# The last batch's two norms and its store, written out apart at the end of the experts stage

## The chip, the cores and the metric

The kernel runs on one core of one Trainium2 chip. The metric is the device time of one execution in microseconds. The kernel before took 1379.23 us (median of three runs, 1375.58 to 1379.28).

## The reference

Four residual blocks run one after the other over x, of 16 batches of 512 tokens of width 128: attention, a gated feed-forward, a state-space block with its own feed-forward, and a mixture of experts. Only the end of the last one matters here:

```python
spikes_moe = sigmoid(output_flat @ c2s_W + c2s_b)
decoded = sigmoid(spikes_moe @ dec_W + dec_b)
y = (decoded - mean(decoded)) * rsqrt(var(decoded) + 1e-5) * ln_g + ln_b
x = x + (y - mean(y)) / sqrt(var(y) + 1e-5)
```

Both means and variances go over the 128 features of a token. `ln_g` and `ln_b` have one value per feature, so they are applied between the two norms.

## The kernel before

Tokens lie on the 128 partitions: a batch is four tiles (NT = 4) of 128 tokens by 128 features, kept in `X[:, u]` (the residual stream) and `Y[:, u + 1]` (what is to be added). Names: PE is the tensor engine, DVE VectorE, ACT ScalarE, POOL GpSimd, SP the queue that issues the stores.

The stage is `experts()`. Each engine has its own program, written as `body(i, ...)` and driven by `rounds()` (L1981): rounds 0 to 3 written out, rounds 4 to 11 in a hardware loop of two rounds a turn, rounds 12 to 19 written out (B = 16). In round i the engines work on several batches at once: batch i is encoded and routed, batch i - 1 goes through its experts, batch i - 2 is decoded (flag `c`) and its first norm is measured, batch i - 3 goes through the affine part and its second norm is measured (flag `shapes`), and batch i - 4 is added and stored (flag `ends`). `parts()` (L1975) turns the flags off at the ends of the stage. So the last batch, u = 15, is decoded in round 17, shaped in round 18, and added and stored in round 19. Within a round the order of each engine's instructions is the order in the code, and semaphores couple the engines.

The path of one batch u from its decode to its store:

- ACT writes the sigmoid of the decoder's output to `Y` (L2110).
- DVE measures the first norm (`moments_of`, L149 to L163): four `bn_stats`, then five small instructions, of which the last writes `var4`.
- POOL turns `var4` into 1/sqrt (`invert`, L202 to L210: a power and a Newton step, five instructions each waiting for the one before) and makes `offsets` = neg * rstd (L236).
- ACT applies scale and offset to the four tiles (`normalise`, L2066).
- POOL multiplies by the gain and adds the bias (`shape`, L2019 and L2022).
- DVE measures the second norm, POOL inverts it and makes offsets, ACT applies them, all as above.
- POOL adds Y to X (`add`, L2013), and SP stores the batch in one DMA of 256 KB (L1998), which the stage's end waits for.

POOL's round has the order: `shape(i - 3)`, `add(i - 4)`, `shaped.invert` and offset of batch i - 3, `decoded.invert` and offset of batch i - 2. ACT's round 17 has the order: `normalise` of batch 14 by its first norm, two spikes activations (L2088), the sigmoid of batch 15 (L2110), and `normalise` of batch 14 by its second norm. DVE's round 17 measures the second norm of batch 14 and then the first of batch 15.

The instruction order that the change touches on POOL:

```python
if shapes:
    shaped.invert(pool, i - 3, shaped.rstd)
    shaped.offset(pool, i - 3)
if c:
    decoded.invert(pool, i - 2, decoded.rstd)
    decoded.offset(pool, i - 2)
```

Of the kernel before, what the change touches and what calls it, by code (L numbers as in the profile page):

```python
# [14 lines left out]
ALU = mybir.AluOpType  # L15
ACT = mybir.ActivationFunctionType
# [38 lines left out]
class Core:  # L55
# [25 lines left out]
    def sem(self, name):  # L81
        return self.ctx.enter_context(self.nc.semaphore(name))
# [1839 lines left out]
def experts(core, I, W, store):  # L1922
# [8 lines left out]
    with ExitStack() as ctx:  # L1931
# [24 lines left out]
        normed, summed = [[sem(f"{n}{k}") for k in ("x", "y", "z")] for n in ("normed", "summed")]  # L1956
        out = store.rearrange("b (c p) d -> p b c d", p=P)
        stored = sem("stored")
        spread_over = lambda a: a[:].unsqueeze(1).to_broadcast([P, NT, D])
        gap_done, share_done, gates_done = sem("gap_done"), sem("share_done"), sem("gates_done")  # L1960

        heard = sem("heard")
        FIRST_XT = 1
        logits_use, dec_use, next_xT_use = (lambda i, k=k: i * 3 + k for k in (2, 3, 4))
        decoded_use = lambda i, a, b: i * 3 + (3 if a else 2 if b else 0)
# [9 lines left out]
        def parts(i):  # L1975

            within = lambda lo, hi: not isinstance(i, int) or lo <= i <= hi
            return dict(a=within(0, B - 1), b=within(1, B), c=within(2, B + 1), more=within(0, B - 2),
                        joins=within(0, B - 4), shapes=within(3, B + 2), ends=within(4, B + 3))

        def rounds(eng, body):  # L1981

            for i in range(4):
                body(i, i % 2, **parts(i))
            with eng.Fori(0, (B - 8) // 2) as j:
                for p in range(2):
                    i = j * 2 + (p + 4)
                    body(i, p, **parts(i))
            for i in range(B - 4, B + 4):
                body(i, i % 2, **parts(i))  # L1990

        @block.sync
        def _(sp):
            def body(i, p, ends, **_):
                if ends:
                    sp.wait_ge(summed[2], i - 3)
                    sp.sem_inc(core.turns, 1)
                    sp.dma_start(out[:, i - 4], X[:, i - 4]).then_inc(stored, 16)  # L1998

            rounds(sp, body)  # L2000
            sp.wait_ge(stored, 16 * B)

        @block.gpsimd
        def _(pool):
            layer_norm = lambda b: pool_norm(core, pool, b, xn, core.xmean, core.xrstd, centred, b + 1, xn_done)
            pool.memset(rT[64:65], 1.0).then_inc(init, 1)
            pool.wait_ge(init, 1)
            pool.memset(gates[:], 0.0).then_inc(init, 1)

            def add(u, k):  # L2010
                pool.wait_ge(normed[k], u + 1)
                pool.sem_inc(core.turns, 1)
                pool.tensor_tensor(X[:, u], X[:, u], Y[:, u + 1], ALU.add).then_inc(summed[k], 1)  # L2013

            def shape(u):
                y = Y[:, u + 1]
                pool.wait_ge(normed[1], u + 1)
                pool.sem_inc(core.turns, 1)
                pool.tensor_tensor(y, y, spread_over(W.gain), ALU.mult).then_inc(summed[1], 1)  # L2019
                pool.wait_ge(summed[1], u * 2 + 1)  # L2020
                pool.sem_inc(core.turns, 1)
                pool.tensor_tensor(y, y, spread_over(W.bias), ALU.add).then_inc(summed[1], 1)  # L2022

            joined.constant(pool, init, 2)
            add(0, 0)
            add(1, 0)
            joined.invert(pool, 0, core.xrstd)
            layer_norm(0)
            joined.invert(pool, 1, core.xrstd)
            add(2, 0)  # L2030
            pool.wait_ge(TP.full, FIRST_XT)
            pool.sem_inc(core.turns, 1)
            layer_norm(1)

            def body(i, p, c, more, joins, shapes, ends, **_):
                if shapes:
                    shape(i - 3)
                if ends:
                    add(i - 4, 2)
                if isinstance(i, int) and i == 0:  # L2040
                    joined.invert(pool, 2, core.xrstd)
                if joins:
                    add(i + 3, 0)
                if more:
                    pool.wait_ge(TP.full, next_xT_use(i))
                    pool.sem_inc(core.turns, 1)
                    if not isinstance(i, int) or i < B - 2:
                        layer_norm(i + 2)
                if shapes:
                    shaped.invert(pool, i - 3, shaped.rstd)  # L2050
                    shaped.offset(pool, i - 3)
                if c:
                    decoded.invert(pool, i - 2, decoded.rstd)
                    decoded.offset(pool, i - 2)
                if joins:
                    joined.invert(pool, i + 3, core.xrstd)

            pool.wait_ge(*W.experts)
            rounds(pool, body)

        @block.scalar
        def _(act):
# [18 lines left out]
            def spikes_encoded(n, m):  # L2081
                EB[m].read(act, n)
                EB[m].emptied(act.activation(enc[:, m], EB[m].t[:], ACT.Sigmoid, bias=W.encb[:, m:m + 1]))
# [8 lines left out]
                    HB[h].read(act, n)  # L2092
                    HB[h].emptied(act.activation(hid[:, 2 * k + h], HB[h].t[:], ACT.Relu))  # L2093

            def body(i, p, a, b, c, more, joins, shapes, **_):
                if a:
                    FB.read(act, cont_use(i))
                    act.activation(rT[0:64], FB.t[router], ACT.Tanh, bias=s2rb[:]).then_inc(heard, 1)
                if shapes:
                    decoded.wait(act, i - 3)  # L2100
                    normalise(i - 3, decoded.rstd, decoded.offsets, normed[1])
                if c:
                    cells_to_spikes(c2s_use(i))
                if joins:
                    normalise(i + 3, rstd, shift, normed[0])
                if b:
                    expert_hidden(hid_use(i, 0), 0)
                if c:
                    TP.read(act, decoded_use(i, a, b))
                    TP.emptied(act.activation(Y[:, i - 1].rearrange("p c d -> p (c d)"), TP.t[:], ACT.Sigmoid))  # L2110
                if b:
                    expert_hidden(hid_use(i, 1), 1)
                if more:
                    take_xT(next_xT_use(i))
                if a:
                    act.wait_ge(gap_done, i + 1)
                    act.activation(share[:], gap[:], ACT.Sigmoid).then_inc(share_done, 1)
                if b:
                    expert_hidden(hid_use(i, 2), 2)
                if more:  # L2120
                    spikes_encoded(next_enc_use(i), 0)
                if b:
                    expert_hidden(hid_use(i, 3), 3)
                if more:
                    spikes_encoded(next_enc_use(i), 1)
                if shapes:
                    shaped.wait(act, i - 3)
                    normalise(i - 3, shaped.rstd, shaped.offsets, normed[2])

            act.wait_ge(W.folded, W.MERGED)  # L2130
            take_xT(FIRST_XT)
            for m in range(HC):
                spikes_encoded(1, m)
            rounds(act, body)

        @block.tensor
        def _(pe):
# [142 lines left out]

        @block.vector
        def _(v):
            tick = Tally(v, steps, per=14)
            wide = lambda a: a.unsqueeze(2).to_broadcast([P, NT, E])
            numbers = W.number.unsqueeze(1).to_broadcast([P, NT, E])

# [31 lines left out]
            def gate(i):  # L2318
                slots = lambda a, n: gates[:, :, a * E:(a + n) * E].rearrange("p c (s e) -> p c s e", e=E)
                copies = lambda n: hit[:].unsqueeze(2).to_broadcast([P, NT, n, E])  # L2320
                v.wait_ge(share_done, i + 1)
                v.tensor_tensor(hit[:], mask[0][:], wide(share[:, 0]), ALU.mult)
                tick.step(v.tensor_tensor(cand[:], mask[1][:], wide(share[:, 1]), ALU.mult))
                tick.step(v.tensor_tensor(hit[:], hit[:], cand[:], ALU.add))
                tick.step(v.tensor_copy(slots(0, 3), copies(3)))
                v.tensor_tensor(hit[:], hit[:], gates[:, :, 0:E], ALU.subtract).then_inc(gates_done, 1)
                v.wait_ge(gates_done, i * PARTS + 1)
                v.tensor_copy(slots(3, 2), copies(2)).then_inc(gates_done, 1)
                v.wait_ge(gates_done, i * PARTS + 2)
                v.tensor_tensor(gates[:, :, 5 * E:6 * E], hit[:], gates[:, :, 3 * E:4 * E], ALU.subtract)\  # L2330
                 .then_inc(gates_done, 1)

            def body(i, p, a, b, c, joins, shapes, **_):
                if a:
# [48 lines left out]
            v.wait_ge(W.shaped, W.SHAPED)  # L2383
            v.wait_ge(init, 2)
            rounds(v, body)


def program(nc, I, out):
# [65 lines left out]
```

## Time and profile before

| | us |
|---|---|
| median of 3 runs | 1379.23 |
| lowest, highest run | 1375.58, 1379.28 |
| the profiled execution, its own time | 1381.35 |
| its span, first to last instruction | 1379.2 |
| last matmul of the kernel (PE L2227) ends | 1357.2 |
| last add on POOL (L2013) ends | 1376.45 |

Busy shares of the span: PE 86%, DVE 69%, ACT 66%, POOL 48%. Times in the rows are microseconds from the start of the span. Engine names with a q behind them (POOLq, SPq) are an engine's sequencer, which issues DMAs and holds waits. "Idle before <- X" says how long an engine stood still before an instruction and what released it.

### The profile page before, as it was taken

How to read it: one execution, taken by the hardware profiler on the slowest of the kernel's cores; microseconds unless marked ns; L12 is line 12 of the kernel's file. 1: busy time of each engine (PE TensorE's matmuls, PEld its weight loads, DVE VectorE, ACT ScalarE, POOL GpSimd, SP SyncE). 2: the span in 40 equal slices, each digit the busy share in tenths (PEclk: the TensorE clock that was granted, in tenths of full speed). 3: DMA queues.
4: the chain of work that ended last, by engine and by line, in shares of the span. 5: the costliest groups of instructions: out<-in, count | busy, mean ns of one | idle time of the engine just before them, and what ended most of it. 6: DMA issues, size and time to landing. Idle time of an engine off the chain costs nothing. (4 is left out here: it accounts for less than half of the span.)

```text
span 1379.2 us, 27741 instructions
## 1 busy us (share of the span) xinstructions
PE 1186.9 (86%) x7410; PEld 529.1 (38%) x7410; DVE 946.4 (69%) x2936; ACT 912.9 (66%) x1373; POOL 668.7 (48%) x1127
## 2 busy tenths in 40 slices
PE   3698999999999999993999568999669999999993
PEld 1122222222222222222656458677423433434431
DVE  3477777777777777673799676566545788888752
ACT  2588999999999999994455590333424666666553
POOL 5444555565555555433355541122242566666545
PEclk8699999999999999996999879999869999999997
DMA  4664565555555555507810011000000000000000
GB/s 119 132 117 90 99 112 108 107 108 102 104 108 105 107 100 100 104 1 191 246 36 0 1 63 62 1 0 0 0 0 0 9 9 15 15 8 16 16 16 23
DMA packets 71177, 87.95 MB, mean 64 GB/s; under 512 B 10136, under 2 KB 64958, under 8 KB 65214
## 3 DMA queue, kind: packets, MB, share of 16 engines
q1 hardware_dynamic: 69078, 85.55, 29.8%
q10 hardware_dynamic: 2024, 1.51, 0.5%
q8 instruction: 33, 0.54, 0.2%
q14 instruction: 42, 0.34, 0.1%
HBM read 63.84 MB, written 31.59 MB: 69 GB/s over the span
## 5 line engine op out<-in xcount | busy, mean ns | idle before, releaser
L511 ACT ACTIVATE a_probs<-a_S 128x1024 f32<-128x1024 f32 x512 | 496.6, 1036 | 74.0 <-DVE a_S L653 66.0
L653 DVE TENSOR_TENSOR a_S<-a_S,a_tables 128x256 f32<-128x256 f32 (+1 forms) x512 | 281.1, 560 | 157.3 <-PE a_S L527 154.4
L534 PE MATMUL a_O<-a_probs,a_V 128*32 128x512 f32 x2048 | 275.1, 609 | 2.4 <-ACT a_probs L511 0.6
L527 PE MATMUL a_S<-a_Qs,a_Ks 48*128 48x512 bf16 x1024 | 180.0, 388 | 26.8 <-DMA a_Qs<-a_parts_dram 13.9
L527 PEld LDWEIGHTS a_S<-a_Qs,a_Ks 48*128 48x128 bf16 x1024 | 42.7, 93 | 242.2 <-ACT a_probs L511 196.1
L2093 ACT ACTIVATE e_hid<-e_H 128x512 f32<-128x512 f32 x128 | 69.5, 595 | 61.5 <-PE e_H L2199 61.5
L431 POOL CAST a_parts<-a_whole 128x512 bf16<-128x512 f32 x47 | 29.1, 620 | 157.6 <-DVE a_whole L663 148.2
L1843 ACT ACTIVATE g_hid<-g_H,w_b 128x512 f32<-128x512 f32 x64 | 44.0, 687 | 84.2 <-PE g_H L1866 84.2
L2197 PE MATMUL e_H<-e_gated,w_We 64*128 64x512 f32 x256 | 74.2, 656 | 1.3 <-ACT e_hid L2093 1.2
L534 PEld LDWEIGHTS a_O<-a_probs,a_V 128*32 128x32 f32 x2048 | 40.4, 108 | 82.6 <-issue 67.4
L2208 PE MATMUL e_O<-e_hid,w_We 128*64 128x512 f32 x256 | 69.5, 615 | 0.4 <-ACT e_hid L2093 0.4
L2300 DVE TENSOR_TENSOR e_gated<-e_contT,e_G 128x512 f32<-128x512 f32 x64 | 43.8, 684 | 25.3 <-PE e_G L2189 25.0
L1866 PE MATMUL g_H<-g_ynT,w_w 128*128 128x512 f32 x128 | 60.4, 617 | 0.9 <-DVE g_ynT L1308 0.9
L1876 PEld LDWEIGHTS g_OUT<-w_w,g_hid 128*128 128x128 f32 x512 | 59.7, 192 | 0.6
L550 PE MATMUL a_M<-ident,a_Osb 128*128 128x128 f32 x256 | 41.8, 286 | 21.1 <-DVE a_xnT L657 17.2
L1876 PE MATMUL g_OUT<-w_w,g_hid 128*128 128x128 f32 x512 | 59.7, 275 | 0.0
L440 POOL TENSOR_TENSOR a_parts<-a_whole,a_parts 128x512 bf16<-128x512 f32 x47 | 54.5, 1161 | 8.6 <-POOL a_parts L437 8.6
L434 POOL TENSOR_TENSOR a_whole<-a_whole,a_parts 128x512 f32<-128x512 f32 x47 | 54.4, 1158 | 8.6 <-POOL a_parts L431 8.6
L1495 PE MATMUL f_OUT<-f_wT,f_hid 128*128 128x128 f32 x384 | 49.4, 288 | 6.1 <-ACT XY L1420 6.1
L202 POOL TENSOR_TENSOR g_power_rstd<-g_power_var,g_power_half (+1 forms) x16 | 16.3, 1018 | 76.7 <-DVE g_power_var L179 76.5
L1495 PEld LDWEIGHTS f_OUT<-f_wT,f_hid 128*128 128x128 f32 x384 | 46.7, 200 | 12.8 <-ACT XY L1420 9.4
L550 PEld LDWEIGHTS a_M<-ident,a_Osb 128*128 128x128 f32 x256 | 26.8, 140 | 56.1 <-issue 30.1
(357 smaller groups left out, 2412.0 us busy)
## 6 DMA issues: line engine op xcount, KB each, us to landing
a_parts_dram<-a_parts SPq DMA_DIRECT2D x94, 192.0 KB, 5.7
a_Qs<-a_parts_dram SPq DMA_DIRECT2D x64, 192.0 KB
a_Qs<-a_parts_dram SPq DMA_DIRECT2D x64, 128.0 KB
m_taps_by_step<-h_taps SPq DMA_DIRECT2D x8, 1024.0 KB, 13.6
m_taps<-m_taps_by_step SPq DMA_DIRECT2D x8, 1024.0 KB, 5.0
a_Ks<-a_parts_dram SPq DMA_DIRECT2D x30, 192.0 KB
XY<-L_attn_x SPq DMA_DIRECT2D x16, 256.0 KB, 7.2
a_Qs<-a_parts_dram SPq DMA_DIRECT2D x64, 64.0 KB
```

What stands on the lines that cost most here:

```text
L440: pool.tensor_tensor(part(2), whole[w][:], part(1), ALU.subtract).then_inc(lowered[w], 1)
L511: act.activation(probs[n % KEPT][:], S[n % RING][:], ACT.Exp).then_inc(exped, 1)
L527: mm = pe.matmul(S[n % RING][:, par, :], Ks[p][rows, pr, kb * P:(kb + 1) * P], Qs[p][Q_OF(kb)][rows, pr, :], start=True, stop=True)
L534: mm = pe.matmul(O[VC * j:VC * (j + 1), :], V[q][:, kb, HG * g + j, :], probs[(2 * m + j // 2) % KEPT][:, j % 2, :], start=(kb == 0), stop ...
L550: mm = pe.transpose(M[:, tile_of(core, c)], src[:, tile_of(core, c)], core.ident[:])
L653: v.tensor_tensor(s[:, :, where], s[:, :, where], wide, ALU.mult).then_inc(corrected, 1)
L1495: mm = pe.matmul(OUT[q].t[:, tile_of(core, c)], hid[q][:, m, tile_of(core, c)], wT[2][:, m, :], start=(m == 0), stop=(m == FC - 1))
L1866: pe.matmul(H[m][:], w1[:, tile_of(core, m)], ynT[p][:], start=True, stop=True).then_inc(h_full, 1)
L1876: mm = pe.matmul(o, hid[p][:, m, tile_of(core, c)], w2[:, m, :], start=False, stop=(m == FC - 1), skip_group_check=True)
L2093: HB[h].emptied(act.activation(hid[:, 2 * k + h], HB[h].t[:], ACT.Relu))
L2197: pe.matmul(HB[h].t[:], W.We1[half[h], k], gated[k % 2][half[h]], start=True, stop=False)
L2208: mm = pe.matmul(OB.t[h * M:(h + 1) * M], W.We2[:, 2 * k + h, :], hid[:, 2 * k + h, :], start=(k == 0 and h == 1), stop=(k == PAIRS - 1), ...
```

## The change

Batch 15 leaves the common rounds after its decode. The rounds end at 18, `shapes` ends with round 17 and `ends` with round 18, and POOL does nothing more for batch 15. In round 17 ACT, behind the sigmoid of batch 15, loads the table for the square root and takes the root of the first norm's variance (`root(0, decoded)`), ahead of its `normalise` of batch 14; the root of the second (`root(1, shaped)`) comes behind the rounds. DVE has a new function `close(15)` behind its rounds: four instructions (y + neg) * gain, a reciprocal of the root, four y * rstd + bias, the measuring of the second norm, four y + neg, a reciprocal, and four y * rstd + x. All of the four-fold ones are 128x128 instructions, one for each tile. SP and ACT each issue one half (two tiles, 128 KB) of the store of batch 15, both waiting for the last of DVE's steps.

```diff
+        GAINED, BIASED, MOVED, CLOSED = (PER * B + n for n in (2, 3, 4, 6))
+        CHAIN = Norm.MEASURE * B
+        roots = sb("roots", [P, 2, NT])
...
-                        joins=within(0, B - 4), shapes=within(3, B + 2), ends=within(4, B + 3))
+                        joins=within(0, B - 4), shapes=within(3, B + 1), ends=within(4, B + 2),
+                        closes=isinstance(i, int) and i == B + 1)
...
-            for i in range(B - 4, B + 4):
+            for i in range(B - 4, B + 3):
...
             rounds(sp, body)
-            sp.wait_ge(stored, 16 * B)
+            sp.wait_ge(steps, CLOSED)
+            sp.dma_start(out[:, B - 1, 0:NT // 2], X[:, B - 1, 0:NT // 2]).then_inc(stored, 16)
+            sp.wait_ge(stored, 16 * (B + 1))
...
-                if c:
+                if c and not closes:
                     decoded.invert(pool, i - 2, decoded.rstd)
                     decoded.offset(pool, i - 2)
...
+                if closes:
+                    act.preload_act_table(ACT.Sqrt)
+                    root(0, decoded)
                 if shapes:
                     shaped.wait(act, i - 3)
                     normalise(i - 3, shaped.rstd, shaped.offsets, normed[2])
+
+            def root(k, norm):
+                act.wait_ge(norm.steps, norm.start + CHAIN)
+                act.activation(roots[:, k], norm.var4[:, B - 1], ACT.Sqrt, scale=0.25).then_inc(normed[1], 1)
...
             rounds(act, body)
+            root(1, shaped)
+            act.wait_ge(steps, CLOSED)
+            act.dma_start(out[:, B - 1, NT // 2:NT], X[:, B - 1, NT // 2:NT]).then_inc(stored, 16)
...
+            def close(u):
+                y, x = Y[:, u + 1], X[:, u]
+                last = Tally(v, steps, start=PER * B)
+                for c in range(NT):
+                    op = v.scalar_tensor_tensor(y[:, c], y[:, c], decoded.neg[:, u, c:c + 1], W.gain[:], ALU.add, ALU.mult)
+                last.mark(op)
+                v.wait_ge(normed[1], B)
+                last.step(v.reciprocal(decoded.rstd[:, u], roots[:, 0]))
+                assert last.start + last.n == GAINED
+                for c in range(NT):
+                    op = v.scalar_tensor_tensor(y[:, c], y[:, c], decoded.rstd[:, u, c:c + 1], W.bias[:], ALU.mult, ALU.add)
+                last.step(op)
+                assert last.start + last.n == BIASED
+                shaped.moments_of(v, u, y)
+                for c in range(NT):
+                    op = v.tensor_scalar(y[:, c], y[:, c], shaped.neg[:, u, c:c + 1], None, ALU.add)
+                last.mark(op)
+                assert last.start + last.n == MOVED
+                v.wait_ge(normed[1], B + 1)
+                last.step(v.reciprocal(shaped.rstd[:, u], roots[:, 1]))
+                for c in range(NT):
+                    op = v.scalar_tensor_tensor(x[:, c], y[:, c], shaped.rstd[:, u, c:c + 1], x[:, c], ALU.mult, ALU.add)
+                last.mark(op)
+                assert last.start + last.n == CLOSED
...
             rounds(v, body)
+            close(B - 1)
```

## Rows read from the trace of the kernel before

**Rows 1.** The page: the chain that ended last, shares of the span by engine.

```profile
DVE 10%; PE 10%; issue 4%; POOL 1%; ACT 1%; DVEq 1%; POOLq 0%; ACTq 0%
```

**Rows 2.** The chain that ended last, 1358 to the end: start us, us, what.

```profile
1358.15 1.03 POOL e_shaped_rstd L202
...
1361.07 0.97 POOL e_decoded_rstd L202
...
1363.94 1.66 ACT XY L2066 x4
...
1365.77 1.27 POOL XY L2019
...
1368.50 0.89 DVE e_shaped_st L149 x4
...
1375.16 1.29 POOLq L1931
```

**Rows 3.** Timeline, 1357 to 1369: start us, us, engine, line, instruction.

```profile
1357.25 0.60 ACT L2110 ACTIVATE XY<-e_TP 128x512 f32<-128x512 f32 x1 [2.30 <-PE e_TP L2227]
...
1357.89 0.86 DVE L149 BATCH_NORM_STATS2 e_decoded_st<-XY 128x6 f32<-128x128 f32 x4
...
1359.33 0.16 DVE L163 SCALAR_TENSOR_TENSOR e_decoded_var<-e_decoded_spread,e_decoded_square 128x4 f32<-128x4 f32 x1
...
1361.10 1.65 ACT L2066 ACTIVATE XY<-XY,e_shaped_offsets,e_shaped_rstd 128x128 f32<-128x128 f32 x4 [3.26 <-POOL e_shaped_offsets L236]
...
1368.42 1.26 POOL L2013 TENSOR_TENSOR XY<-XY 128x512 f32<-128x512 f32 x1
```

**Rows 4.** Stores and other DMAs: issue ns, KB each, us from issue to landing.

```profile
L1998 SPq DMA_DIRECT2D out<-XY x16: 378/380/416, 1096.6 to 1376.5; - x16
...
DMA to landing us min/median/max: 2.3/2.3/2.3
a_parts_dram<-a_parts ACTq DMA_DIRECT2D x2, 192.0 KB, 2.8
XY<-L_attn_Wk ACTq DMA_DIRECT2D x1, 64.0 KB, 2.1
```

**Rows 5.** DVE on 128x128 operands: one line's durations (ns min/median/max), two timeline groups.

```profile
L738 DVE SCALAR_TENSOR_TENSOR XY<-XY x15: 339/343/593, 94.0 to 113.8; 128x128 f32<-128x128 f32 x15
643.45 1.10 DVE L1516 TENSOR_SCALAR f_xn<-XY,xmean,xrstd 128x128 f32<-128x128 f32 x4
859.84 0.87 DVE L1887 TENSOR_SCALAR g_yn<-XY,g_power_rstd 128x128 f32<-128x128 f32 x4 [0.32 <-POOL g_power_rstd L210]
```

**Rows 6.** Groups by shape, DVE: a reciprocal (busy us, mean ns | idle before).

```profile
L715 DVE RECIPROCAL XY<-XY 128x16 f32<-128x16 f32 x1 | 0.2, 247 | 0.0
```

**Rows 7.** Timeline of ACT around two table loads, and the work behind each.

```profile
779.99 1.28 ACT L1451 ACT_TABLE_LOAD   x1
...
795.24 10.88 ACT L1701 ACTIVATE m_u<-XY,in_rstd,urstd 128x128 f32<-128x128 f32 x28 [1.92 <-DVE in_mean L1754]
992.25 1.28 ACT L2071 ACT_TABLE_LOAD   x1
...
993.54 4.72 ACT L2066 ACTIVATE XY<-XY,e_shift,e_rstd 128x128 f32<-128x128 f32 x12
```

**Rows 8.** Timeline of POOL and DVE at two places where their work overlaps.

```profile
1323.13 1.27 POOL L2013 TENSOR_TENSOR XY<-XY 128x512 f32<-128x512 f32 x1
1323.25 1.19 DVE L2309 SCALAR_TENSOR_TENSOR e_cand<-e_hit,w_table 128x32 f32<-128x32 f32 x1
92.20 1.04 POOL L99 TENSOR_TENSOR a_xn<-XY,in_mean 128x512 f32<-128x512 f32 x1 [0.27 <-POOL in_rstd L210]
92.69 0.63 DVE L736 TENSOR_SCALAR XY<-XY 128x128 f32<-128x128 f32 x1
```

**Rows 9.** One line's durations (ns min/median/max), and one of the page's instruction queues.

```profile
L2309 DVE SCALAR_TENSOR_TENSOR e_cand<-e_hit,w_table x32: 191/191/1278, 1016.9 to 1325.6; 128x32 f32<-128x32 f32 x32
q8 instruction: 33, 0.54, 0.2%
```

More of the change, by code:

```diff
@@ L1958, in experts @@
         stored = sem("stored")
+        PER = 14
         spread_over = lambda a: a[:].unsqueeze(1).to_broadcast([P, NT, D])
@@ L2033, in _, with body @@
             layer_norm(1)
-            def body(i, p, c, more, joins, shapes, ends, **_):
+            def body(i, p, c, more, joins, shapes, ends, closes, **_):
                 if shapes:
@@ L2093, in expert_hidden, with body @@
                     HB[h].emptied(act.activation(hid[:, 2 * k + h], HB[h].t[:], ACT.Relu))
-            def body(i, p, a, b, c, more, joins, shapes, **_):
+            def body(i, p, a, b, c, more, joins, shapes, closes, **_):
                 if a:
@@ L2282, in _ @@
         def _(v):
-            tick = Tally(v, steps, per=14)
+            tick = Tally(v, steps, per=PER)
             wide = lambda a: a.unsqueeze(2).to_broadcast([P, NT, E])
```

## The prediction

> **What bounds the kernel now.** I read the page first. Its chain of work that ended last gives PE and DVE a tenth of the span each and POOL and ACT a hundredth each [rows 1]: the end of the kernel is small beside the rest, and nothing the change does can be worth more than that end. So I went to the same chain in order of time, from 1358 us on [rows 2]. The last matmul is over at 1357.2, and from there only DVE, ACT and POOL pass one batch from hand to hand: POOL begins to invert batch 15's first norm at 1361.07, ACT applies it at 1363.94, POOL does gain and bias from 1365.77 on, DVE measures the second norm at 1368.50, and POOL's final add goes from 1375.16 to 1375.16 + 1.29 = 1376.45. No other work stands between these steps. The timeline [rows 3] shows where the handing over starts: ACT's sigmoid of batch 15 ends at 1357.25 + 0.60 = 1357.85, and DVE has its first variance ready at 1359.33 + 0.16 = 1359.49. Everything before 1359.49 is the same in both kernels. From there to 1376.45 are 16.96 us, and the store and the end of the program take 1379.2 - 1376.45 = 2.75 us more, of which 2.3 are the store's way from issue to landing [rows 4]. These 19.7 us are all that the change can touch.
>
> **What goes.** Batch 15's inversions on POOL (each a power of about 1.0 us and five short steps, 2.9 us in all, 1361.07 to 1363.94), the wait of the first one behind the inversion of batch 14 (1359.49 to 1361.07), two four-tile passes on ACT of 1.65 us, and three POOL passes of about 1.27 us, one of which, the bias, had also to run before DVE could measure.
>
> **What comes, on DVE.** The trace has the same form, a `scalar_tensor_tensor` of 128x128 with a per-partition scalar and two inputs in SBUF: line 738, median 343 ns [rows 5]. It never stands there four in a row. The nearest group of four, with two per-partition scalars, takes 1.10 us for four where one takes about 336 ns, so one starts every 0.255 us; I take 1.10 us for each group of four. The `tensor_scalar` group with one scalar takes 0.87 us [rows 5]. The lower bound for a group is 0.87, the upper is four unoverlapped, 4 x 0.343 = 1.37. The reciprocal of 128x4 is not in the trace; the one of 128x16 takes 247 ns [rows 6], that is its upper bound, and I take 0.2. Step by step:
>
> - The first group starts behind the variance's issue, at 1359.41, and ends at 1359.41 + 1.10 = 1360.51.
> - The reciprocal runs to about 1360.65. It waits for ACT's root. ACT is free at 1357.85, the table load takes 1.28 [rows 7] and ends at 1359.13, the root waits for 1359.49 and is done by 1359.75: 0.7 us of cover. If this cover were gone, each 0.1 us would count in full.
> - y * rstd + bias: to 1361.75, and 0.03 to see it written: 1361.78.
> - The second norm is measured as the first one was, 1357.89 to 1359.49 = 1.60 us [rows 3]: 1363.38.
> - The four y + neg start with the variance's issue, 1363.30 + 0.87 = 1364.17. ACT's second root (0.2 us) lies beside them, behind ACT's pass over batch 14, which ends at 1361.10 + 1.65 = 1362.75 [rows 3].
> - Reciprocal to 1364.31, the last four to 1365.41.
>
> That is 1376.45 - 1365.41 = 11.04 us earlier, if nothing is in DVE's way.
>
> **What is in its way.** POOL's add of batch 14, which before ran at 1368.42 behind the gain and bias of batch 15 [rows 3], now waits only for ACT's pass, and so starts at about 1362.75 + 0.18 = 1362.93, right in DVE's close. Rows show what that does: an add of POOL from 1323.13 to 1324.40 held a DVE instruction with two SBUF inputs, started at 1323.25, until 1324.44, 1.19 us instead of the line's median 0.191 [rows 8, 9]; a one-input `tensor_scalar` of 128x128 was held in the same way, 92.69 to 93.32, by POOL's work to 93.24 [rows 8]. The neg of the second norm, which has two inputs, is due 1.6 - 0.16 - 0.27 = 1.17 us behind 1361.78, at 1362.95, just as the add sets in. In the rows the held instructions began 0.15 to 0.2 us before the recorded end of POOL's (1324.44 - 0.19 = 1324.25; 93.32 - 0.28 = 93.04), so the neg would begin at about 1364.19 - 0.17 = 1364.02, **1.07 us** late, and all behind it. If the add came a little later it would hit y + neg or the last four instead, at about the same price, as all of them are of the forms held in the rows. Lower bound 0 (DVE is first each time, or the add falls on `bn_stats`), upper 1.26, one add. The close then ends at 1366.48.
>
> The Trainium skill, page "SBUF — State Buffer", section "Who interferes with whom", has a rule that speaks against this change: a DVE instruction with two SBUF inputs and a GpSimd instruction that reads SBUF lock each other out for a whole instruction, and whoever comes first wins. The rows above show one direction. No row here shows POOL held up by DVE.
>
> **Elsewhere on the queues.** ACT's table load and first root stand ahead of its pass over batch 14. That pass started at 1361.10, and ACT is free again at 1359.75, so it hides them with 1.35 us to spare. The pass uses Identity: after the load for the square root at 779.99 ACT ran Identity passes with no second load [rows 7], so I count none. The Trainium skill, page "ScalarE: Activation LUTs", section "What ACT_TABLE_LOAD costs", gives about 1.38 us of drain on top of the load, 2.66 us in all. Here the trace disagrees: the load at 992.25 ends at 993.53 and the next pass starts at 993.54 [rows 7]. By the page the first root would come at about 1360.75, DVE's reciprocal 0.3 us late, and the gain 0.3 us smaller. The sum goes by the row.
>
> The store: SP has its store of batch 14 (issue 0.38 us) ahead of the half, issued near 1364.3 and out of the way. The two halves of 128 KB move the same bytes at once. No row has a 128 KB store; a 64 KB load takes 2.1 us and a 192 KB store from ACT's queue 2.8, against 2.3 for the whole batch [rows 4]. So the halves gain at most 0.2 us and lose at most 0.5; nearest is the 256 KB store itself, and I take 0 and leave the 2.75 us as they are.
>
> **Sum.** 11.04 - 1.07 = 9.97, say **10.0 us** earlier. The profiled execution took 1381.35 us, of which 1379.2 span and 2.15 around it; it becomes 1371.35. The median of the runs lies 2.12 below that execution, so the forecast for the median is 1379.23 - 10.0 = **1369.2 us**, 0.7% less. A measurement of this kernel can tell about 0.3%, 4.1 us, from no change.
>
> **The rivals.**
>
> 1. No collision: the gain is 11.0, 1368.2 us. For it: the neg and the add meet within 0.02 us in my sum, and either could win; against: the add has then still y + neg and the last four to meet. Chance 0.22.
> 2. The lock works both ways. POOL's short steps for batch 14, which end at 1361.07 now [rows 2], then have to find room between DVE's two groups; only the stretch of `bn_stats` from 1361.78 is free. The offset comes at about 1362.7, ACT's pass ends at 1364.4, the second root is done at 1364.65, 0.5 us after DVE could have used it, and the add of batch 14 meets the last four. DVE ends near 1366.8, or POOL's add ends at 1367.0 and SP issues batch 14's store ahead of the last half. The gain is 8.7 to 9.7; at 9.2, 1370.0 us. For it: the same lock; against: POOL's power of about 1.0 us at 1358.15 [rows 2] did not hold DVE's small two-input instructions up to 1359.49. By the rule of the Trainium skill cited above (whoever comes first wins), this is what happens if DVE is first. Chance 0.20.
> 3. No difference that can be measured: DVE's groups cost their upper bounds (3 x 0.27 more), the add collides, the halves lose 0.5, and some 4 us of fetching or waiting come that I don't see; 1375 to 1379. Chance 0.04.
> 4. **Slower: the straight code is fetched late.** The place is the close on DVE, some 36 instructions executed once, behind a loop. The price of one stop is at least that of a small transfer, 2.1 us [rows 4]. It decides from the point at which the stops cost more than 10.0 + 4.1 = 14.1 us, seven in a row: 1383.9 us. Against it: the first instruction queue needed 33 packets for the whole kernel [rows 9], and rounds 12 to 19 are straight code too and show no such gap on the chain. Chance 0.02. With 0.01 for the runs' own scatter this gives 0.03 for slower.
> 5. That the change does not do what it says: the last four could run while the end is set elsewhere, but the chain shows no other work behind 1357.2 than batches 14 and 15, so it is part of rival 2.
>
> **How the numbers follow.** The forecast has 0.51, rivals 1 and 2 have 0.42, all of them faster by over 0.3%; 0.04 for the same, 0.03 for slower. The range takes the gains from 8.7 to 11.0 and the scatter of the runs: low 1375.58 - 11.0 = 1364.6, high 1381.35 - 8.7 = 1372.7.
>
> **What would show it.** In the profile after: (a) DVE's variance of batch 15's first norm at 1359.5, then a close of 6.0 to 7.1 us; (b) groups of four at 1.10 and 0.87 us; (c) one table load of 1.28 us on ACT ending before DVE's first group does, and no second one; (d) the add of batch 14 within the close, and one DVE instruction beside it of over 1 us; (e) 2.75 us from the last DVE instruction to the end. The prediction is wrong if the span shrinks by less than 8.7 us, if DVE waits for a root, or if POOL's add is the last work before the store.

## The result and the profile after

The changed kernel took 1368.46 us (median of five runs, 1367.31 to 1371.03), the kernel before 1379.28 (five runs, 1375.58 to 1380.87). The ratio is 0.9928, with a 95% interval from 0.9914 to 0.9942: 9.9 us faster, between 8.0 and 11.9. The profiled execution took 1368.46 us, with a span of 1366.4 us, 12.8 us less than the one before.

The chain that ended last, from 1355 us to the end, is all DVE now, but for 0.26 us of DVE's sequencer (start us, us, what); in the kernel before POOL, ACT and DVE took turns there [rows 2]:

```profile
1356.57 0.16 DVE e_decoded_var L163
1356.73 1.05 DVE XY L2354 x4
1357.78 0.10 DVE e_decoded_rstd L2357
...
1357.90 1.15 DVE XY L2360 x4
...
1359.08 0.88 DVE e_shaped_st L149 x4
...
1360.53 0.16 DVE e_shaped_var L163
1360.69 1.79 DVE XY L2365 x4
1362.48 0.10 DVE e_shaped_rstd L2369
...
1362.60 0.35 DVE XY L2371
1362.95 0.26 DVEq L1931
1363.22 0.52 DVE XY L2371 x2
```

The timeline of the same stretch shows what the other engines did beside it:

```profile
1355.09 1.28 ACT L2134 ACT_TABLE_LOAD   x1
...
1356.57 0.16 DVE L163 SCALAR_TENSOR_TENSOR e_decoded_var<-e_decoded_spread,e_decoded_square 128x4 f32<-128x4 f32 x1
...
1356.65 1.13 DVE L2354 SCALAR_TENSOR_TENSOR XY<-XY,e_decoded_neg,w_gain 128x128 f32<-128x128 f32 x4
1356.77 0.20 ACT L2142 ACTIVATE e_roots<-e_decoded_var 128x4 f32<-128x4 f32 x1 [0.40 <-DVE e_decoded_var L163]
1356.98 0.34 POOL L206 TENSOR_TENSOR e_shaped_work<-e_shaped_work,e_shaped_var 128x4 f32<-128x4 f32 x1 [0.18 <-POOL e_shaped_work L204]
...
1357.70 0.17 DVE L2357 RECIPROCAL e_decoded_rstd<-e_roots 128x4 f32<-128x4 f32 x1
1357.90 1.14 DVE L2360 SCALAR_TENSOR_TENSOR XY<-XY,e_decoded_rstd,w_bias 128x128 f32<-128x128 f32 x4
...
1358.50 0.35 POOL L236 TENSOR_TENSOR e_shaped_offsets<-e_shaped_neg,e_shaped_rstd 128x4 f32<-128x4 f32 x1 [0.18 <-POOL e_shaped_rstd L210]
1358.88 1.65 ACT L2073 ACTIVATE XY<-XY,e_shaped_offsets,e_shaped_rstd 128x128 f32<-128x128 f32 x4 [1.90 <-POOL e_shaped_offsets L236]
...
1360.61 1.87 DVE L2365 TENSOR_SCALAR XY<-XY,e_shaped_neg 128x128 f32<-128x128 f32 x4
1360.70 1.31 POOL L2020 TENSOR_TENSOR XY<-XY 128x512 f32<-128x512 f32 x1 [1.86 <-ACT XY L2073]
1360.73 0.20 ACT L2142 ACTIVATE e_roots<-e_shaped_var 128x4 f32<-128x4 f32 x1 [0.20 <-DVE e_shaped_var L163]
...
1362.60 1.14 DVE L2371 SCALAR_TENSOR_TENSOR XY<-XY,e_shaped_rstd 128x128 f32<-128x128 f32 x4
1363.77 0.38 SPq L2007 DMA_DIRECT2D out<-XY  x1
1363.77 0.48 ACTq L2151 DMA_DIRECT2D out<-XY  x1
```

To compare profiles whose earlier parts differ, I measure the **tail**: from the start of DVE's last small step of batch 15's first norm (L163, `e_decoded_var`) to the end of the last compute instruction. Before it was 1376.45 - 1359.33 = 17.12 us, after 1363.74 - 1356.57 = 7.17. That is 9.95 us. The other 2.8 us between the two spans were there before the experts stage began: ACT's first table load of that stage starts at 990.19 us in the trace of before and at 987.44 in the one of after.

### The profile page after: what moved, and what is told of

Its sections match the earlier page's. It is cut to its first block and busy times, and to the rows that moved or that the text cites. A ratio compares the mean times of both kernels' runs of the same rounds, so it can differ in the third digit from the quotient of the medians.

```text
span 1366.4 us, 27724 instructions
## 1 busy us (share of the span) xinstructions
PE 1184.5 (87%) x7410; PEld 527.6 (39%) x7410; DVE 951.3 (70%) x2954; ACT 910.8 (67%) x1368; POOL 662.1 (48%) x1112
```

## The experiments

### Is the gain all in the tail?

The changed kernel was run again, and the kernel before was profiled again. The pieces of code from here on are parts of each edit, and ... stands for lines not shown.

> The changed kernel once more, as the measure for the others. In its first profile the tail from the start of DVE's last small step of batch 15's first norm (L163) to the last DVE instruction took 1363.74 - 1356.57 = 7.17 us, against 1376.45 - 1359.33 = 17.12 in the kernel before: 9.95 of the 12.8 us by which the spans differ. The other 2.8 us lie ahead of the experts stage. Theory (the change is worth its tail, the rest is scatter between executions): the tail is again 7.1 to 7.3 us, and the ratio to the kernel before 0.991 to 0.994. Rival (the new code also changes the earlier stages by some 2.8 us): the tail is the same, and the ratio 0.990 to 0.991 with the experts stage again starting near 987.4 instead of 990.2.

> The kernel before once more, for a second profile of it. Theory (the 2.8 us of difference between the first two profiles ahead of the experts stage are scatter): its experts stage starts anywhere from 987 to 993 us, its tail is again 17.1 us to within 0.05. Rival (the changed code also makes the earlier stages faster): it starts at 990 or later.

Measured: the changed kernel 1370.39 us against 1380.22, ratio 0.9926 (0.9909 to 0.9944), tail 1368.30 - 1361.13 = 7.17 us. Its experts stage began at 992.04 us. The kernel before, in its second profile, began that stage at 988.73 and had a tail of 1374.68 - 1357.56 = 17.12 us. Over the twelve profiles of this study the stage begins anywhere from 986.8 to 992.9 us, with either kernel. So the tail repeats to 0.01 us, the stages ahead scatter by 6 us, and the extra 2.8 us of the first pair of profiles belong to this scatter. What makes it was not looked into.

### What does POOL's add of batch 14 cost DVE?

A memset of four columns stands in the place of the add, so this kernel leaves out the last sum of batch 14.

```diff
-                if ends:
+                if ends and isinstance(i, int) and i == B + 2:
+                    pool.wait_ge(normed[2], B - 1)
...
+                    pool.memset(hit_free[:], 0.0).then_inc(summed[2], 1)
+                elif ends:
                     add(i - 4, 2)
```

> POOL's add of batch 14 (L2020 in the changed kernel) is replaced by a memset of 4 columns, so batch 14's last sum is left out. Theory (this add holds DVE's y + neg group, 1.87 us instead of 0.87): the group takes 0.87 to 0.90, the tail shrinks from 7.17 to 6.1 to 6.25 us. Rival (the group of four tensor_scalar is slow by itself in this place, because it writes in place or is fetched late): it stays at 1.8 to 1.9 and the tail at 7.1 to 7.2.

The tail was 1365.46 - 1359.29 = 6.17 us, 1.00 shorter, and the group y + neg is back at 0.87 us in its timeline:

```profile
1363.33 0.87 DVE L2370 TENSOR_SCALAR XY<-XY,e_shaped_neg 128x128 f32<-128x128 f32 x4
1363.39 0.10 POOL L2049 MEMSET e_hit_free<- 128x4 f32 x1 [1.84 <-ACT XY L2078]
```

The rival (the group is slow by itself) falls. The median, 1368.04 us (1364.38 to 1373.01), can't tell 1 us from the scatter; the timeline can.

### Does DVE hold POOL up as well?

DVE's close is held back until POOL has the offsets of batch 14.

```diff
                 y, x = Y[:, u + 1], X[:, u]
+                shaped.wait(v, B - 2)
                 last = Tally(v, steps, start=PER * B)
```

> DVE begins its close only when POOL has the offsets of batch 14, so that POOL's short steps run alone. Theory (the lock works both ways, and DVE's groups stretch these steps from 0.20 to 0.30 to 0.35 us): all four steps and the offset are back at 0.20 us, the offset ends 1.74 us behind L163's start as in the kernel before instead of 2.28, the group y + neg is back at 0.87 to 1.0 because the add of batch 14 now falls earlier, on the second group or the bn_stats, and one of those is held instead if it has two inputs. The tail becomes 7.17 + 1.7 = 8.3 to 9.2 us. Rival (the steps are long for another reason): they stay at 0.30 to 0.35.

POOL's steps are short again, and the add now meets DVE's second group (timeline):

```profile
1357.40 0.20 POOL L206 TENSOR_TENSOR e_shaped_work<-e_shaped_work,e_shaped_var 128x4 f32<-128x4 f32 x1 [0.18 <-POOL e_shaped_work L204]
...
1358.53 0.20 POOL L236 TENSOR_TENSOR e_shaped_offsets<-e_shaped_neg,e_shaped_rstd 128x4 f32<-128x4 f32 x1 [0.18 <-POOL e_shaped_rstd L210]
1358.77 1.14 DVE L2355 SCALAR_TENSOR_TENSOR XY<-XY,e_decoded_neg,w_gain 128x128 f32<-128x128 f32 x4 [1.61 <-POOL e_shaped_offsets L236]
...
1360.03 2.14 DVE L2361 SCALAR_TENSOR_TENSOR XY<-XY,e_decoded_rstd,w_bias 128x128 f32<-128x128 f32 x4
1360.59 1.43 POOL L2020 TENSOR_TENSOR XY<-XY 128x512 f32<-128x512 f32 x1 [1.86 <-ACT XY L2073]
...
1363.74 0.87 DVE L2366 TENSOR_SCALAR XY<-XY,e_shaped_neg 128x128 f32<-128x128 f32 x4
```

All as the theory had it: the offset ends 1358.73 - 1356.99 = 1.74 us behind L163's start instead of 1358.85 - 1356.57 = 2.28, the tail is 1365.87 - 1356.99 = 8.88 us. Two things more can be read. The first group, now with no POOL step beside it, takes 1.14 us, as much as the two groups of the changed kernel that have two or three such steps beside them (1.13 and 1.14), so POOL's short steps cost DVE nothing; it is POOL that pays, 0.10 to 0.15 us for each of four. And when POOL's add starts inside a running DVE group, both are longer: 1.43 us instead of 1.26, and 2.14 instead of 1.14.

### What are the two halves of the change worth, roots and passes?

First the passes alone: POOL inverts, DVE does the rest, and ACT's table load and roots are gone.

```diff
...
-                v.wait_ge(normed[1], B)
-                last.step(v.reciprocal(decoded.rstd[:, u], roots[:, 0]))
+                v.wait_ge(decoded.inverted, Norm.INVERT * B)
+                last.step(v.tensor_copy(roots[:, 0], decoded.rstd[:, u]))
...
```

> The two inverted roots of batch 15 come from POOL again (power and Newton step), DVE's passes stay; a small copy stands where the reciprocal was. Theory (root on ACT and reciprocal on DVE are worth what POOL's chain costs, about 3.3 us at the first norm, where it stands behind batch 14's inversion, and about 1.5 to 2.5 at the second): the tail is 11.7 to 12.8 us, so 4.6 to 5.6 us longer than in the changed kernel, and the time about 1373.5. Rival (DVE's passes carry nearly all of the gain, the roots are hidden behind the first group): the tail is under 9.5 us.

The tail was 1370.51 - 1357.73 = 12.78 us, the time 1375.21, ratio 0.9961 (0.9948 to 0.9974). The waits stand in the timeline, 3.32 us for the first inversion and 2.03 for the second, and the add of batch 14 met the second group (2.23 us instead of 1.14):

```profile
1362.26 0.17 DVE L2355 COPY e_roots<-e_decoded_rstd 128x4 f32<-128x4 f32 x1 [3.32 <-POOL e_decoded_rstd L210]
1362.46 2.23 DVE L2358 SCALAR_TENSOR_TENSOR XY<-XY,e_decoded_rstd,w_bias 128x128 f32<-128x128 f32 x4
...
1369.16 0.17 DVE L2367 COPY e_roots<-e_shaped_rstd 128x4 f32<-128x4 f32 x1 [2.03 <-POOL e_shaped_rstd L210]
```

Then the roots alone, built on the kernel before. One thing more changes here: ACT passes batch 15 by its first norm ahead of batch 14 by its second, where the kernel before has it the other way round.

```diff
...
+                if isinstance(i, int) and i == B + 1:
+                    act.preload_act_table(ACT.Sqrt)
+                    root(0, decoded)
+                    decoded.wait(act, B - 1)
+                    normalise(B - 1, decoded.rstd, decoded.offsets, normed[1])
...
+            def root(k, norm):
+                act.wait_ge(norm.steps, norm.start + Norm.MEASURE * B)
+                act.activation(roots[:, k], norm.var4[:, B - 1], ACT.Sqrt, scale=0.25).then_inc(rooted, 1)
...
+            def turn(k, norm):
+                v.wait_ge(rooted, k + 1)
+                v.reciprocal(norm.rstd[:, B - 1], roots[:, k]).then_inc(turned, 1)
+                v.wait_ge(turned, k + 1)
+                v.tensor_tensor(norm.offsets[:, B - 1], norm.neg[:, B - 1], norm.rstd[:, B - 1], ALU.mult).then_inc(norm.moved, 1)
```

> The kernel before with the roots alone changed: ACT takes the roots of batch 15, DVE the reciprocal and the offset, ACT's passes, POOL's gain, bias and add and the single store stay. ACT passes batch 15 by its first norm ahead of batch 14's second pass. Theory (the two parts of the change add up, about 5.6 us of its 9.95 for the roots by the run before, the rest for the passes): the tail from L163's start to the last add is 17.12 less 5.5 to 6.5 = 10.6 to 11.6 us, time about 1373.5 to 1374.5. Rival (each part alone brings little, because the other then sets the end): the tail is over 14 us.

The tail was 1366.90 - 1355.97 = 10.93 us, the time 1374.52 us (1371.78 to 1380.93), ratio 0.9969 (0.9954 to 0.9983). By the ratio that is 4.3 us, between 2.3 and 6.3, so the 6.19 us by which the tail is shorter lie at the edge of what the runs allow. The hand-overs it shortened, in its timeline:

```profile
1356.17 0.20 ACT L2141 ACTIVATE e_roots<-e_decoded_var 128x4 f32<-128x4 f32 x1 [0.40 <-DVE e_decoded_var L163]
...
1356.41 0.18 DVE L2388 RECIPROCAL e_decoded_rstd<-e_roots 128x4 f32<-128x4 f32 x1 [0.27 <-ACT e_roots L2141]
1356.62 0.16 DVE L2390 TENSOR_TENSOR e_decoded_offsets<-e_decoded_neg,e_decoded_rstd 128x4 f32<-128x4 f32 x1
...
1356.82 1.65 ACT L2068 ACTIVATE XY<-XY,e_decoded_offsets,e_decoded_rstd 128x128 f32<-128x128 f32 x4 [0.44 <-DVE e_decoded_offsets L2390]
...
1357.52 0.20 POOL L236 TENSOR_TENSOR e_shaped_offsets<-e_shaped_neg,e_shaped_rstd 128x4 f32<-128x4 f32 x1 [0.18 <-POOL e_shaped_rstd L210]
1358.37 1.63 ACT L2068 ACTIVATE XY<-XY,e_shaped_offsets,e_shaped_rstd 128x128 f32<-128x128 f32 x4
```

From a tail of 17.12, the passes alone save 4.34 us, the roots alone 6.19, both 9.95. Their sum would be 10.53, so the parts add up but for 0.6 us. Taken back from the changed kernel instead, the roots are worth 12.78 - 7.17 = 5.61 us and the passes 10.93 - 7.17 = 3.76. But the 6.19 hold ACT's new order too. In the old order batch 15's pass would have had to stand behind batch 14's, whose offsets are ready at 1357.72; one pass starts 1358.37 - 1356.82 = 1.55 us behind the other, so it would have started near 1359.3 instead of 1356.82. An estimate from these rows is that about 2.5 of the 6.19 us are the order and some 3.7 the roots themselves, less than the passes alone. No run separates the two. What is shown is that the roots on top of the passes bring 5.61 us, more than the passes alone.

### And the store in two halves?

One store in the changed kernel (ACT's half is taken out), and two halves in the kernel before:

```diff
-            sp.dma_start(out[:, B - 1, 0:NT // 2], X[:, B - 1, 0:NT // 2]).then_inc(stored, 16)
-            sp.wait_ge(stored, 16 * (B + 1))
+            sp.dma_start(out[:, B - 1], X[:, B - 1]).then_inc(stored, 16)
+            sp.wait_ge(stored, 16 * B)
```

> The changed kernel with one store of 256 KB from SP for batch 15. In the changed kernel the end of the span comes 1366.44 - 1363.74 = 2.70 us behind the last DVE instruction, in the kernel before 2.75 behind the last add. Theory (halves change next to nothing): 2.65 to 2.8 us from DVE's end to the end of the span, the tail 7.17. Rival (the halves save what half of the bytes take): 2.9 to 3.2 us.

```diff
+            act.wait_ge(summed[2], B)
+            act.dma_start(out[:, B - 1, NT // 2:NT], X[:, B - 1, NT // 2:NT]).then_inc(stored, 16)
```

> The kernel before with batch 15's store in two halves from SP and ACT, nothing else. Theory: the end comes 2.65 to 2.8 us behind the last add, as with one store. Rival (two halves save): 2.3 to 2.5 us.

Measured from the last compute instruction to the end of the span, in one profile of each: one store 1371.95 - 1369.24 = 2.71 us in the changed kernel (1366.44 - 1363.74 = 2.70 with halves), halves 1377.33 - 1374.57 = 2.76 us in the kernel before (1379.22 - 1376.45 = 2.77 with one store). Halves issued together are worth nothing. The changed kernel's issues and landings show why: SP's half lands after 1.9 us, ACT's, issued at the same time, only after the 2.3 us that a whole batch takes (KB each, us to landing). In the kernel before with halves, where ACT's was issued 0.06 us ahead, it was ACT's that landed after 2.1 us and SP's after 2.3:

```profile
out<-XY SPq DMA_DIRECT2D x1, 256.0 KB, 2.3
out<-XY SPq DMA_DIRECT2D x1, 128.0 KB, 1.9
out<-XY ACTq DMA_DIRECT2D x1, 128.0 KB, 2.3
```

### A version that uses what was found

POOL's add of batch 14 was cut into tiles, each started behind ACT's pass of its tile, and SP's half of the store was released two tiles early:

```diff
+                    for n in range(NT):
+                        pool.wait_ge(tiled, n + 1)
...
+                        op = pool.tensor_tensor(X[:, B - 2, n], X[:, B - 2, n], Y[:, B - 1, n], ALU.add)
...
-            sp.wait_ge(steps, CLOSED)
+            sp.wait_ge(steps, HALF)
```

> The changed kernel with POOL's add of batch 14 cut into its four tiles, each started as soon as ACT has passed its tile, and with SP's half of the last store released when DVE has done the first two tiles. Theory (what an add costs DVE is only the part of it that falls on instructions with two SBUF inputs or on tensor_scalar; on bn_stats it is free): the first add falls on bn_stats, the others on the small steps and the first of y + neg, DVE loses 0.3 to 0.8 us instead of 1.00, and the tail is 6.5 to 7.0 us; from DVE's end to the end of the span 2.3 to 2.7 us. Rival (each POOL instruction costs DVE anew, so that cutting makes it worse): the tail is 7.2 us or more.

The tail was 1364.03 - 1357.29 = 6.74 us and the end came 1366.33 - 1364.03 = 2.30 us later; the time was 1368.7, ratio 0.9907 (0.9874 to 0.9941). The first add falls on `bn_stats`, which isn't held. The adds start at 1360.26, 1360.68, 1361.09 and 1361.5 and take 0.46 us each. All five small steps have two inputs in SBUF, but only the three issued well inside an add are held: L154, L158 and L163 take 0.45, 0.31 and 0.30 us instead of 0.17, 0.17 and 0.16. L155 and L161, issued less than 0.1 us before an add ends, are not. The three make 0.56 of the 6.74 - 6.17 = 0.57 us by which this tail is longer than the one without the add:

```profile
1359.80 0.87 DVE L149 BATCH_NORM_STATS2 e_shaped_st<-XY 128x6 f32<-128x128 f32 x4
1360.26 1.70 POOL L2050 TENSOR_TENSOR XY<-XY 128x128 f32<-128x128 f32 x4 [0.70 <-ACT XY L2148]
1360.70 0.45 DVE L154 TENSOR_TENSOR e_shaped_diff<-e_shaped_st 128x4 f32<-128x4 f32 x1
...
1361.26 0.31 DVE L158 SCALAR_TENSOR_TENSOR e_shaped_neg<-e_shaped_diff,e_shaped_st 128x4 f32<-128x4 f32 x1
...
1361.68 0.30 DVE L163 SCALAR_TENSOR_TENSOR e_shaped_var<-e_shaped_spread,e_shaped_square 128x4 f32<-128x4 f32 x1
1361.90 0.86 DVE L2378 TENSOR_SCALAR XY<-XY,e_shaped_neg 128x128 f32<-128x128 f32 x4
```

On top of that, y + neg of two of the four tiles was given to ACT:

```diff
+            for n in range(NT // 2, NT):
+                y = Y[:, B, n]
+                act.activation(y, y, ACT.Identity, bias=shaped.neg[:, B - 1, n:n + 1]).then_inc(shifted, 1)
```

> The kernel of the last run, with y + neg of tiles 2 and 3 moved to ACT, behind its second root. DVE has two of four left before its reciprocal, and ACT's two passes (0.39 us apart) end about 1.2 us behind the variance, while DVE's last group reaches tile 2 about 1.2 us and tile 3 1.5 us behind it. Theory: 0.3 to 0.45 us less than the last run, tail 6.1 to 6.6 us, and with it 3 us at most below the changed kernel, likely 1, which the runs cannot tell from it: ratio to the kernel before 0.990 to 0.993. Rival (ACT's pass comes too late and DVE waits for it): the tail is no shorter than in the last run.

The tail was 1363.84 - 1357.50 = 6.34 us, and the end again 1366.15 - 1363.84 = 2.31 us later (in both versions ACT's half, issued 0.5 us behind SP's, now lands in 1.9 us, so halves that are released apart do save 0.4 us). Tail and end together are 8.65 us against 7.17 + 2.70 = 9.87 in the changed kernel: 1.2 us less. The time was 1368.62, ratio 0.9916 (0.9887 to 0.9945), which the runs can't tell from the changed kernel. Both versions beat the kernel before; that they beat the changed one is shown by the tail alone.

## Why the prediction was right

The forecast was 1369.2 us, against 1368.46; the gain of 10.0 us stands against 9.95 in the tail and 9.9 in the ratio. Step by step:

- **Groups of four.** 1.10 us forecast, 1.13 and 1.14 measured. L1516, two per-partition scalars on one input, was a good stand-in for one scalar on two inputs. The `tensor_scalar` group is 0.87, as forecast, when nothing is in its way.
- **Reciprocal.** 0.2 forecast, 0.16 to 0.17 measured.
- **Cover of the first root.** The load ended at 1356.37, the root at 1356.97, the reciprocal was due at 1357.70: 0.7 us of cover, as forecast. The root starts 0.40 us after the load's end, released by DVE's variance (1356.73). The 1.38 us of drain of the Trainium skill, page "ScalarE: Activation LUTs", section "What ACT_TABLE_LOAD costs", would have put it at 1357.75; the trace decides against it. No second load came, so Identity ran on the root's table.
- **The collision.** Forecast 1.07 us, measured 1.00, by taking the add away. Its place was off by one step: I had the add begin 3.60 us behind L163's start and hit the neg, it began 4.13 us behind it (1360.70) and hit y + neg. The cause is what rival 2 named and the sum put at nothing: DVE's groups stretch POOL's short steps, and with them ACT's pass and the add come 0.54 us later. The price of rival 2 did not come, though. POOL was not shut out for a group but got in between DVE's instructions at 0.10 to 0.15 us a step, 0.54 us in all, and a later add cost DVE the same.
- **Rival 1** (no collision) had the two within 0.02 us of each other. It failed by the same 0.54 us: the neg was safe, the next group was not.
- **The store.** 0 forecast, within 0.01 us of 0 measured, in both kernels.
- **Close and end.** 7.15 us from L163's start to DVE's end forecast (1366.48 - 1359.33), 7.17 measured; 2.75 behind it forecast, 2.70 measured. Two errors offset each other in the close: without the collision it takes 6.17 us where the sum had 1365.41 - 1359.33 = 6.08, and the collision cost 0.07 less than forecast.
- **Slower by late fetching.** The chain has the one piece of 0.26 us of DVE's own sequencer inside the last group, but the group takes 1.14 us like the others, so no fetch is to be seen.

That the median came within 0.8 us of the forecast is partly luck: the spans of the two profiles of the changed kernel, 1366.4 and 1371.0 us, differ by 4.6 us, all of it ahead of the tail. What the sum could get right was the tail.

## What to carry to other kernels

When one last item runs through three engines, count the hand-overs: putting its whole end on one engine saved 10 us of 17 here, and with the passes already there, taking the scalars between them from POOL (where DVE waited 2.03 and 3.32 us for power and Newton step) brought another 5.6 of the 10. When one part of a change is tried alone, look whether its test also changes the order of an engine's work: here that may be 2.5 us of the 6.19. Before moving work onto DVE, look for POOL work that this move sets free to start earlier: it will land beside the moved work, and in these traces it cost where DVE's instructions had two SBUF inputs or were `tensor_scalar`, but not on `bn_stats`. Changes under 0.3% are to be read in a repeatable stretch of the trace, not in the medians.

## What the runs showed of the hardware

- POOL and DVE held each other up in both directions, and unequally: a 128x512 add on POOL cost a DVE group 1.00 to 1.09 us, a 128x4 step cost it nothing and was itself held for 0.10 to 0.15 us by a stream of DVE instructions. The Trainium skill, page "SBUF — State Buffer", section "Who interferes with whom", has the lock; the trace agrees that it works in both directions, and adds that a stream of DVE instructions 0.26 us apart does not keep POOL out.
- Cutting a 128x512 add of POOL into four tiles took 1.70 us instead of 1.26 to 1.31, and still cost DVE less, 0.57 us (6.74 - 6.17) instead of 1.00, because one tile fell on `bn_stats` and only three of the small steps were held.
- The kernel before shows the same of `bn_stats`: its add of batch 14 ran from 1368.42 to 1369.68 [rows 3] beside all four of them, which took 0.87 us as ever, and held only the small step behind them, 0.30 us instead of 0.17. So this add cost DVE 0.13 us before the change and 1.00 after it:

```profile
1368.50 0.87 DVE L149 BATCH_NORM_STATS2 e_shaped_st<-XY 128x6 f32<-128x128 f32 x4 [9.01 <-POOL XY L2022]
1369.40 0.30 DVE L154 TENSOR_TENSOR e_shaped_diff<-e_shaped_st 128x4 f32<-128x4 f32 x1
```

- Two stores of 128 KB issued together land after 1.9 and 2.3 us; 0.5 us apart they take 1.9 each.
